# Windowed attention on 64-row tiles of TensorE, layer norm on ScalarE, and the norm's root on POOL, in a six-layer transformer kernel

## The reference, cut to what matters

```python
HEADS, DIM_HEAD, WINDOW = 16, 64, 32
for i in range(6):
    x = attn_layer(shift_tokens(x), Wqkv[i], q_scale[i], k_scale[i], Wo[i]) + x
    x = ffn_layer(shift_tokens(x), ln_g[i], ln_b[i], W1[i], b1[i], W2[i], b2[i]) + x
# attn_layer: q = l2norm(q) * qs, k = l2norm(k) * ksc, both rotated, then local_attention:
#   the 256 tokens are cut into 8 windows of 32; the 32 queries of a window see
#   64 keys, those of their own window and of the window before it
sim = jnp.einsum('bhwie,bhwje->bhwij', bq, bk2) * QK_SCALE      # 32 x 64 per head and window
attn = jax.nn.softmax(jnp.where(mask, -max, sim), -1)
out = jnp.einsum('bhwij,bhwje->bhwie', attn, bv2)
# ffn_layer: layer norm of 128 channels, 128 -> 2 x 341, a * gelu(gate), 341 -> 128, + b2
```

## Time and profile before

| | us |
|---|---|
| median of 3 runs (1964.91 to 1966.18) | 1965.3 |
| the profiled execution | 1965.16 |
| its span, first to last instruction | 1963.4 |
| PE busy in the span | 1874.6 |
| DVE, ACT, POOL busy | 1643.9, 1390.9, 1378.3 |

### The profile page before, as it was taken

One profiled execution on the slowest core, in us unless ns is written; L12 is line 12 of the kernel. 1 busy time (PEld: TensorE's weight loads), 2 busy tenths in 40 slices (PEclk: granted clock), 3 DMA queues, 4 the chain that ended last, 5 costly groups with the idle time before them and its releaser, 6 DMA issues. The chain is left out here.

```text
span 1963.4 us, 54531 instructions
## 1 busy us (share of the span) xinstructions
PE 1874.6 (95%) x21027; PEld 1510.2 (77%) x21027; DVE 1643.9 (84%) x3362; ACT 1390.9 (71%) x2676; POOL 1378.3 (70%) x1394
## 2 busy tenths in 40 slices
PE   7999868999999999999999999999999999999996
PEld 5888747778777877887787788778778877877874
DVE  5887757898898888889888988988898898889873
ACT  4777736776777677777767777777777677677762
POOL 4777757776877677777768767777776687676661
PEclk8999989999999999999999999999999999999998
DMA  4000011110111111110101211011111101110100
GB/s 133 2 1 2 1 45 42 34 36 21 52 45 49 31 30 30 55 50 23 49 21 30 65 33 50 21 39 56 44 28 40 30 21 39 32 51 20 38 22 22
DMA packets 46293, 70.32 MB, mean 36 GB/s; under 512 B 15567, under 2 KB 29781, under 8 KB 46037
## 3 DMA queue, kind: packets, MB, share of 16 engines
q1 hardware_dynamic: 44564, 64.73, 11.3%
q10 hardware_dynamic: 1472, 2.10, 0.3%
HBM read 21.72 MB, written 1.05 MB: 12 GB/s over the span
## 5 line engine op out<-in xcount | busy, mean ns | idle before, releaser
L1094 POOL TENSOR_TENSOR ra<-ra,rb 128x512 f32<-128x512 f32 x384 | 487.6, 1282 | 70.1 <-DVE rb L1090 68.3
L1132 POOL TENSOR_TENSOR qn<-ra,rs 128x512 f32<-128x512 f32 x384 | 394.2, 1049 | 53.7 <-DVE rs L1125 53.7
L1206 POOL TENSOR_TENSOR pr<-pr,rl 128x512 f32<-128x512 f32 x192 | 200.4, 1044 | 268.2 <-DVE rl L1200 268.2
L1069 DVE TENSOR_REDUCE ss<-sq 128x8 f32<-128x512 f32 x384 | 259.5, 676 | 16.8 <-ACT sq L1058 11.6
L1196 DVE TENSOR_REDUCE sm<-pr 128x8 f32<-128x512 f32 x192 | 130.4, 679 | 13.9 <-ACT pr L1192 13.9
L1192 ACT ACTIVATE pr<-dif 128x512 f32<-128x512 f32 x192 | 121.5, 633 | 21.9 <-PE pT L1212 13.8
L1222 ACT COPY pt<-pT 64x512 f32<-64x512 f32 x144 | 83.0, 577 | 64.8 <-PE pT L1212 64.0
L1337 DVE TENSOR_SCALAR early<-fx,fmv,frs 128x128 f32<-128x128 f32 x96 | 69.5, 783 | 43.0 <-POOL frs L322 43.0
L1240 PE MATMUL pS<-pt,vs 128*64 128x64 f32 x1536 | 101.8, 229 | 0.4 <-ACT pt L1222 0.4
L1240 PEld LDWEIGHTS pS<-pt,vs 128*64 128x64 f32 x1536 | 77.4, 137 | 29.5 <-issue 28.5
L492 POOL TENSOR_TENSOR ra<-ra,rb 128x512 f32<-128x512 f32 x64 | 81.5, 1291 | 24.9 <-DVE rb L488 24.9
(11 more groups left out here) (346 smaller groups left out, 6224.6 us busy)
## 6 DMA issues: line engine op xcount, KB each, us to landing
vs<-v SPq DMA_DIRECT2D x96, 384.0 KB, 3.3
wqkvA<-in_L_ffn_Wqkv SPq DMA_DIRECT2D x18, 512.0 KB, 5.0
vs<-v SPq DMA_DIRECT2D x96, 64.0 KB, 3.0
woB<-in_L_ffn_Wo SPq DMA_DIRECT2D x6, 512.0 KB, 4.0
w<-in_L_ffn_W SPq DMA_DIRECT2D x6, 341.0 KB, 2.9
out<-x SPq DMA_DIRECT2D x4, 256.0 KB, 2.3
x<-in_L_attn_x SPq DMA_DIRECT2D x1, 768.0 KB, 8.2
w<-in_L_ffn_W SPq DMA_DIRECT2D x12, 64.0 KB
```

What stands on the lines that cost most here:

```text
L1069: e.tensor_reduce(ss[:, j, :], sq[:, j % 2, :].rearrange("p (h d) -> p h d", d=DB), AX.X, ALU.add).then_inc(b_ss.sem, 1)
L1094: e.tensor_tensor(ra[:, j, :], ra[:, j, :], rb[:, j % 2, :], ALU.add).then_inc(b_ad.sem, 1)
L1132: e.tensor_tensor(qn[:, j % 4, :].rearrange("p (h d) -> p h d", d=DB), ra[:, j, :].rearrange("p (h d) -> p h d", d=DB), rs[:, c % 2, 8 * j ...
L1206: e.tensor_tensor(y, y, rl[:, s, :].unsqueeze(2).to_broadcast([P, 8, 64]), ALU.mult).then_inc(b_pn.sem, 1)
```

## The change

**Scores.** `qd` is replaced by `qT` without zeros. `scores` is called for a group `g`, not a unit: two masks into two banks, then for every head pair, window and half one matmul on 64 rows (one head), with 32 weight columns (32 queries) and 64 moving columns. The two heads of a pair lie in row halves and write into a bank each; four windows lie in four strips of 32 partitions. There are 64 matmuls where two units had 32.

**Values.** `pt` is plain, with a slot for each unit. `values` has 16 matmuls on 64 rows with 64 weight columns and 32 moving columns, in place of 8 on 128 rows with 64 moving columns; the two window parities lie in row halves with a bank each. The four calls of a group stand together.

**Copies.** `turn_copy` of q and `copy_p` are one full-height copy each. **Softmax** has four buffers (`sp`, in place) instead of two. **Root.** `norm_step` has 12 steps; 0 and 1 stay on DVE, 2 to 11 (seven two-input and three one-input instructions) run on POOL. **Layer norm.** `l_norm` is four ACT instructions, `l_root` on POOL gets two more small ones. **b2** is a row of `w2` against a row of ones in `gT`, so `l_bias` is gone. **x.** `xt_copy` is gone; `xt_turn` reads `xr` itself and waits for `f_x`. The weights `w2` are loaded on SP before `move_values(e, l, 3, 0)` instead of after it. The bank tables and all four pair orders are new.

```diff
-        qd = [sb(f"qd{g}", [P, 4, NW, 2 * WIN]) for g in range(GROUPS)]
+        qT = [sb(f"qT{g}", [P, 4, T]) for g in range(GROUPS)]
...
-            for p2 in range(2):
-                for w in range(NW):
-                    lo = p2 * 256 + (w // 2) * 64
-                    i = e.matmul(o[64 * (w % 2):64 * (w % 2) + 64, lo:lo + 64],
-                                 qd[g][:, 2 * s + p2, w, :],
-                                 kT[g][:, 2 * s + p2, WIN * w:WIN * w + 2 * WIN],
+            for k in range(4):
+                for a in range(2):
+                    lo = (2 * k + a) * 2 * WIN
+                    for j in range(4):
+                        w = 4 * (j // 2) + 2 * a + j % 2
+                        for h in range(2):
+                            r = slice(64 * h, 64 * h + 64)
+                            i = e.matmul(o[h][WIN * j:WIN * j + WIN, lo:lo + 2 * WIN],
+                                         qT[g][r, k, WIN * w:WIN * w + WIN],
+                                         kT[g][r, k, WIN * w:WIN * w + 2 * WIN],
...
+            for j in range(4):
+                lo = k * P + j * WIN
+                for h in range(2):
+                    f = k * P + 64 * h
+                    for a in range(2):
+                        r = slice(64 * a, 64 * a + 64)
+                        i = e.matmul(o[a][64 * h:64 * h + 64, lo:lo + WIN], (v if j % 2 else vs)[g][r, j // 2, f:f + 64],
+                                     pt[r, g, h, lo:lo + WIN], start=(k == 0 and j == 0), stop=True,
+                                     skip_group_check=True)
...
-            elif n == 4:
-                e.scalar_tensor_tensor(t, t, -10.0 / 3.0, t, ALU.add, ALU.mult).then_inc(b_rs.sem, 1)
+            elif n == 4:
+                e.tensor_scalar(p, t, -10.0 / 3.0, None, ALU.add).then_inc(b_rs.sem, 1)
+            elif n == 5:
+                e.tensor_tensor(t, t, p, ALU.mult).then_inc(b_rs.sem, 1)
...
+                i = e.activation(fln[:, t, :], fx[:, t, :], ACT.Identity, bias=fnb[:, t:t + 1], scale=frs[:, t:t + 1])
```

More of the change, by code:

```diff
@@ L36 @@
 I32 = mybir.dt.int32
-NORM = 9
+NORM = 12
 ROOM = (1024.0 / 27.0) ** 2
@@ new lines, in turn_copy, with scores @@
+            e.copy(dst, w.rearrange("p (h q) -> p h q", h=4)).then_inc(b_tc.sem, 1)
+        def scores(e, l, c, g):
+            it = l * B + c
+            e.wait_ge(b_tc.sem, b_tc.at(it, 4 * g + 3))
+            o = [banks[SCORE_BANK[c % 2][2 * g + h]] for h in range(2)]
+            for h in range(2):
+                e.matmul(o[h], ident16[:, :], maskB[:, :], start=True, stop=False, skip_group_check=True)
+            for k in range(4):
[8 more added lines that the diff above has]
+                                         kT[g][r, k, WIN * w:WIN * w + 2 * WIN],
+                                         start=False, stop=True, skip_group_check=True)
@@ L1220, in copy_p @@
-            src = groups(banks[TURNP_BANK[c % 2][u]])
-            for h in range(2):
-                i = e.copy(dst[64 * h:64 * h + 64, :, h, :], src[64 * h:64 * h + 64, :, :])
-            i.then_inc(b_pc.sem, 1)
-        def values(e, l, c, k):
-            it = l * B + c
-            u, g, p2, pair = k // 2, k // 4, k % 2, k % 4
-            if p2 == 0:
-                e.wait_ge(b_pc.sem, b_pc.at(it, u))
-            if pair == 0:
+            e.wait_ge(b_pv.sem, b_pv.at(it - 1, 4 * g + 3))
@@ L1236, in values @@
-            for t in range(NT):
-                for par in range(2):
-                    for h in range(2):
-                        lo = pair * P + 64 * h
-                        i = e.matmul(o[64 * h:64 * h + 64, t, :, par, :], (v if par else vs)[g][:, t, lo:lo + 64],
-                                     pt[:, u % 2, 2 * p2 + t, par, :, WIN * h:WIN * h + WIN],
-                                     start=(p2 == 0 and t == 0 and par == 0), stop=True, skip_group_check=True)
+            o = [banks[VALUE_BANK[c % 2][2 * g + a]] for a in range(2)]
@@ L1629, in pair_pe @@
                 l_shift(e, l, p - 1)
-            if on(p - 2):
-                second_layer(e, l, p - 2, 1)
+            if on(p):
+                e.wait_ge(b_sub.sem, b_sub.at(l * B + c, 2))
+                turn_p(e, l, c, 0)
+                e.wait_ge(b_tc.sem, b_tc.at(l * B + c + 1, 1))
+                turn_p(e, l, c, 1)
+                e.wait_ge(b_pc.sem, b_pc.at(l * B + c, 0))
+                turn(e, l, c + 1, 2)
+                e.wait_ge(b_sub.sem, b_sub.at(l * B + c, 3))
+                e.wait_ge(b_pc.sem, b_pc.at(l * B + c, 1))
+                values(e, l, c, 0)
+                e.wait_ge(b_tc.sem, b_tc.at(l * B + c + 1, 0))
+                turn(e, l, c + 1, 3)
+                values(e, l, c, 1)
+                values(e, l, c, 2)
+                values(e, l, c, 3)
             if on(p - 1):
@@ L1998, in pair_pool @@
             if on(p):
+                normalise(e, l, c + 1, 4)
+                soft_norm(e, l, c, 2)
                 soft_norm(e, l, c, 3)
-                normalise(e, l, c + 1, 0)
-                normalise(e, l, c + 1, 1)
-                normalise(e, l, c + 1, 2)
-                normalise(e, l, c + 1, 3)
-                normalise(e, l, c + 1, 4)
-            if on(p - 1):
-                l_root(e, l, p - 1)
+                rotate_add(e, l, c + 1, 6)
+                normalise(e, l, c + 1, 5)
+                normalise(e, l, c + 1, 6)
+                rotate_add(e, l, c + 1, 7)
+            if on(p) and last(p):
+                split_low(e, l + 1, 1, 2)
+            if on(p):
+                normalise(e, l, c + 1, 7)
         def stream(e, pair):
@@ L2081, in dve_program @@
             barrier(e, 0)
-            for g in range(GROUPS):
-                i = e.memset(qd[g][:, :, :, :], 0.0)
-            i.then_inc(b_z.sem, 1)
+            e.memset(gT[64:P, 2, :], 1.0)
             e.wait_ge(e_rb.sem, e_rb.at(0))
```

890 lines of the change are left out of this document (417 added, 473 removed).

## The result

The changed kernel takes 2013.08 us (median of 4 runs, 2007.68 to 2020.7); the kernel before, beside it, 1965.28 (1964.91 to 1966.18). The ratio is 1.0245, 95% interval 1.0212 to 1.0279: slower, where 1865 was forecast, and outside the range of 1835 to 1975. The profiled execution has a span of 2018.9 us.

The account below looks back on a forecast made before the run. PE's own queue was taken as the bound. Per pair, scores −4.7, values −0.7 and new waits +1.0 gave −4.4 us; over 22.7 pairs −100 us, from 1965.3 to 1865 us, range 1835 to 1975.

Parts of the forecast that it names:

- Values: PE's values: four calls together stay at 2.01 us, a pair goes from 8.7 to 8.0 us, a gain of 0.7.
- term for scores: PE's scores: eight tiles run at once, 1.64 us a group with masks, 6.6 us a pair, a gain of 4.7.
- the slips: New PE waits on other engines that earlier slack hid, such as POOL's longer root chain: 1.0 us a pair charged.
- The rival of the slower side: PE's instruction rate bounds scores and values: above 16 ns each the change loses, 2265 us at 29 ns; chance 0.19.
- the estimate of 2174 us: Scores and values at the skill's 25 ns minimum between starts: 9.2 us more a pair.
- Four tiles only: Only four tiles work at once in scores: 1.87 us a group, 1926 us in all; chance 0.15.
- POOL holds the pair: PE gets faster but POOL's queue sets the pair at 64.5 to 66.5 us: 1877 to 1922 us; chance 0.2.
- The marks I had set: PE timeline signs: 128 score instructions in about 1.1 us, PE above 96% busy; 1.9 means four tiles, over 2.7 the rate.

Follow-up runs that it names:

- half the instructions: Changed kernel with half as many matmuls in scores (128 moving columns, not 64) and values (128, not 32), some products not the attention's: 1869.3 us.
- small additions: Changed kernel with the rotation's addition on POOL cut to 128 of its 512 columns: 1990.7 us.
- old values: Changed kernel with values as before (block-diagonal probabilities, two half copies on ACT) and the new scores: 1998.5 us.

## Why the prediction was wrong, point by point

**The step that failed is the price of 128 small matmuls in a row.** In the term for scores I argued from neighbours: two starts 0.02 us apart, eight tiles need a start every 7 ns, so 128 take the streaming time. The first half is right: starts are 7 to 10 ns apart and all eight tiles work. But a unit takes 1.41 us undisturbed, not 1.09 (starts 10.0 ns apart on average, 1013.14 to 1014.41, and 0.14 us to the next work), and 1.96 in the mean, because its 256 instructions are one whole block of supply used in 1.4 us, while blocks can come no faster than one in 3.3 to 4.0. Half of the 81 units between 400 and 1850 us still take 1.41 to 1.44 us, on instructions that were at hand; the others take up to 6.3. Values were right undisturbed (2.00 against 2.01) and 2.48 in the mean. A start distance between two neighbours says what PE can do with instructions that it has; it says nothing about how fast they come.

**In the sum**, per pair: scores 4 x (1.96 − 1.09) = +3.5, so −1.2 instead of −4.7. Values: three groups in a row at 2.48, one split into 0.62 and 1.91, 9.97 against 8.0: +2.0, so +1.3 instead of −0.7. With the slips of 1.0 that gives +1.1. Measured is 47.8 / 22.7 = +2.1 by the medians, and +2.9 in the profiled executions between 400 and 1850 us (1450 / 20.4 against 1450 / 21.3; the profiled one is the longest of its four). Of the 1.8 between +1.1 and +2.9, 0.6 are the waits marked "issue" at other lines (L1361, L977 and smaller ones, 12.4 us over 20.4 pairs). It isn't the slips: the waits of PE that name an engine come to 33.8 us, 1.7 a pair against 0.6 before, which is 1.1 more where 1.0 was charged. The rest fits the lower clock, for which the sum had no term. Work outside scores and values fills 53 us of its 61.4 us; at full clock it would take half as long, so the clock costs some 26 us, 1.3 a pair. This is an estimate from the rows; together the terms give +3.0.

**The 144 us** between the changed kernel and the one with half the instructions divide in the same way, again as estimates: longer units and calls even without a pause, (0.32 + 0.09) x 4 = 1.6 us a pair, 37 us; the pauses inside runs, 75 / 20.4 x 22.7 = 83 us; the pauses at other lines, 14; the lower clock, about 30. That is 20 us more than there is, and the kernel with half the instructions waits longer for other engines (2.2 us a pair against 1.7), which takes back about 11 of them.

**The rest of the sum held.** The kernel with half the instructions is nearly the one that I had in mind: scores 1.09 (forecast 1.09), values 1.91 (2.0), and 1869.3 us for 1865. Its pair takes 64.0 us between 400 and 1800 us, 4.3 less than before, where 4.4 less was forecast. Behind the near hit are two misses that offset each other in part: values gain 0.9 and not 0.7, and its PE idles 47.9 us in these 1400, 2.2 a pair, where before had 12.0, 0.6 a pair. So the slips are 1.6 us, not 1.0. These terms add up to −4.0; the last 0.3 stay open.

**The rival of the slower side** had the right sign and the right subject, the rate at which PE takes instructions, but as one rate for all of them: below 16 ns a gain, at 29 ns 2265 us. Both numbers turn up, 10 ns in a run and 29 in the long average, and neither decides: the time is set by blocks of 256, and only by those used up faster than the next can come. The Trainium skill, TensorE: Matmul & The Clock Gate, section Wait — 56ns, not 53.3ns?, has start-to-start never below about 25 ns; this case's trace disagrees, with 10.0 ns over 128 matmuls on eight tiles, so the estimate of 2174 us by that rule failed too. I gave the rival 0.19 on the thought that the rows of before excluded most of it. They did not: the stretch with the densest instructions in them has 32 in 1.09 us, and a unit of scores is now 128 in 1.4.

**Four tiles only** is out: a unit would take 1.9 us at the least, and takes 1.41. (That the mean is 1.96 is chance: half of the single units lie at 1.41 to 1.44, the others anywhere from 1.55 to 6.3.) The Trainium skill, TensorEngine Tiling (Array Packing), section Tiling Modes, agrees with the trace: eight independent tiles of 64x32.

**POOL holds the pair** was a small part: the small additions give 22 us back, and PE's waits for POOL at its `turn` are 18 us in 1450 in the kernel with half the instructions. Its busy time came out a little under the forecast: 1119.1 us over 20.4 pairs (163 of L1199 in the stretch, 8 a pair) are 54.9 a pair for 56.3. The rows of POOL in the changed kernel, with the columns of the earlier trace rows:

```profile
L1199 POOL TENSOR_TENSOR sp<-sp,rl 128x512 f32<-128x512 f32 x163 | 168.6, 1044 | 91.4 <-DVE rl L1194 91.4
...
L1103 POOL TENSOR_TENSOR nt<-nt,sx 128x64 f32<-128x64 f32 x82 | 26.4, 322 | 34.7 <-DVE nt L1100 31.5
L1105 POOL TENSOR_TENSOR nt<-nt 128x64 f32<-128x64 f32 x82 | 26.3, 321 | 6.4
L1107 POOL TENSOR_SCALAR nt<-nt 128x64 f32<-128x64 f32 x41 | 15.4, 377 | 3.6
```

A root step is 0.32 us (forecast 0.306) and a one-input one up to 0.38, more than a two-input one (taken at 0.28), with 0.08 between them (0.09). The wait for the inverse fell to 91.4 us, 4.5 a pair, from the 11.1 a pair (170 / 8 pairs) of the kernel before in the same stretch, and to 22.0 us in 1400, 1.0 a pair, with half the instructions. That fits the four softmax buffers freeing POOL, though no run changes them alone. The row of before:

```profile
L1206 POOL TENSOR_TENSOR pr<-pr,rl 128x512 f32<-128x512 f32 x170 | 177.4, 1044 | 236.4 <-DVE rl L1200 236.4
```

**DVE** came to 1081.2 / 20.4 = 53.0 us a pair (53.4). **ACT** came to 45.7 and not 43, and I had missed why:

```profile
L1377 ACT ACT_TABLE_LOAD x42 | 53.9, 1283 | 0.8
L1186 ACT ACT_TABLE_LOAD x41 | 52.6, 1283 | 0.8
...
L1335 ACT ACTIVATE early<-fx,fnb,frs 128x128 f32<-128x128 f32 x84 | 35.8, 550 | 0.0
```

Before, there are 21 and 21 loads in that stretch; the new order puts an exponent between the GELUs, so that the table changes twice as often: 21 and 20 more, 2.6 us a pair. And `l_norm` with a scale and a bias for each partition takes 0.55 us, not the 0.37 of the row that I had taken. Neither is on PE's path here; with the old values it would be.

**The marks I had set**: "1.1 us a unit and PE above 96% busy" failed (1.41, and 1340.64 / 1450 = 92.5%). "Over 2.7 us is the rate, 1.9 is four tiles" was too coarse, because it took a unit for something with one length. The mark that would have served is the word "issue" in the waits of PE.

## What to carry to other kernels

When a change cuts work into more and smaller instructions, count them in the densest stretch and not over the kernel: here blocks of 256 instructions of PE (128 matmuls with their loads) came no faster than one in 3.3 to 4.0 us. A row of small matmuls that uses a block faster than that lives on what is at hand, and then PE stands still: not each time, but by 0.55 us a unit on average here. The whole kernel's average, one block in 7.6 us, looks harmless. And count a pause twice: behind 14 of the longer ones the clock fell, and the work that follows ran at half speed. If PE's idle time is marked "issue" inside one line's run, look there first, and compare with a version of half the instructions and no fewer columns before any engine's order is touched. And a rewritten order is a measured thing: breaking the runs up took 40 to 80% of the gaps away each time, and lost more to banks held longer.

## What the runs showed of the hardware

- PE's instructions arrive in blocks of 256 (16 KB), one in 3.5 to 4.0 us when asked for without pause, 14.6 ns an instruction. Up to 223 matmuls ran before the first gap, so nearly two blocks can be at hand. While a layer's parameters were loaded in small packets, one block took 7.0 us instead of 3.7; in the changed kernel the longest gap, 4.55 us before a start at 1402.18, lies in such a load too (two cases, no test).
- The granted clock fell to 0.50 in 14 stretches of the changed kernel (61.4 of 1450 us), each behind a pause of 1.8 us or more without instructions, and never in the same 1450 us of the kernel before, nor up to 1800 us with half the instructions.
- Eight tiles of 64x32 start 7 ns apart at first, 10.0 ns on average over 128 matmuls of 64 columns with their loads.
- Leaving and entering small tiles costs 0.17 us each time (2 x 0.79 against 1.41).
- The kernels with most of the gaps scatter more: 2007.7 to 2020.7 and 2035.6 to 2050.6 us over four runs each, against 1867.6 to 1870.6 with half the instructions and 1964.9 to 1966.2 before.
- On POOL, 64 columns cost 0.32 us with two inputs and 0.29 to 0.38 with one.
